# Factorization-machine attention on one core: first and final products of a pair group in one pass of eight 64-row by 32-column products, the finals carried through the relu as a positive and a negative part, and six SyncE tiles in place of seven

## The reference, cut to what matters

```python
B, N_DENSE, N_FIELDS, VOCAB, EMBED_DIM, ATT_DIM = (2048, 13, 26, 12500, 32, 8)
FIRST, SECOND = np.triu_indices(N_FIELDS, k=1)                  # 325 pairs of fields
emb = jax.vmap(lambda tbl, idx: tbl[idx], in_axes=(0, 1), out_axes=1)(embed_tables, sparse)
bi = emb[:, FIRST, :] * emb[:, SECOND, :]                       # pair products, 32 values each
a = jax.nn.relu(jnp.einsum('bpd,dh->bph', bi, att_w_w) + att_w_b)
scores = jnp.einsum('bph,ho->bpo', a, att_d_w) + att_d_b
att_weight = jax.nn.softmax(scores, axis=1)
att_out = jnp.sum(att_weight * bi, axis=1)
x = jnp.concatenate([att_out, dense], axis=-1)
out = jax.nn.sigmoid(x @ fin_w + fin_b)
```

## Time and profile before

| what | value |
|---|---|
| median of 3 runs | 469.24 us (468.34 to 469.72) |
| profiled execution | 468.43 us |
| its span (first to last instruction) | 466.6 us |
| granted TensorE clock, mean | 0.955 |
| busy PE, PEld, DVE | 399.1, 223.0, 395.3 us |
| busy ACT, POOL | 129.7, 332.4 us |
| POOL gathers | 345 indirect DMAs |
| SP row DMAs | 896 |

### The profile page before, as it was taken

The page is one execution under the profiler, slowest core; times in us unless marked ns, Lnnn a source line. Parts: engine busy times, 40 slices in busy tenths (PEclk is TensorE's granted clock), DMA queues, the critical chain, the costliest instruction groups (busy, mean ns, idle before and its releaser), DMA issues.

```text
span 466.6 us, 9661 instructions
## 1 busy us (share of the span) xinstructions
PE 399.1 (86%) x2508; PEld 223.0 (48%) x2508; DVE 395.3 (85%) x641; ACT 129.7 (28%) x302; POOL 332.4 (71%) x349
## 2 busy tenths in 40 slices
PE   1696969999898987899898899699998899699674
PEld 1585746544336654354326766345326755352121
DVE  4999798999768886999795988899796997898765
ACT  3203311242342111142352121042263111125163
POOL 5877777777777777777777777777777777777600
PEclk9978879999999999799999999899999999899988
DMA  8558323222222222232112243323112223322200
GB/s 294 90 151 161 26 13 26 17 26 15 14 15 26 27 15 26 14 26 16 15 15 15 28 22 27 15 26 16 15 15 14 14 13 17 13 16 16 14 1 1
DMA packets 16535, 15.46 MB, mean 33 GB/s; under 512 B 8192, under 2 KB 15584, under 8 KB 16096
## 3 DMA queue, kind: packets, MB, share of 16 engines
q0 software_dynamic: 11040, 5.67, 23.0%
q1 hardware_dynamic: 3056, 6.80, 4.2%
q10 hardware_dynamic: 2384, 2.37, 2.1%
HBM read 14.79 MB, written 0.02 MB: 32 GB/s over the span
## 4 chain that ended last, share of the span: by engine, by line
SPq 69%; issue 25%; PE 2%; DVE 2%; DMA 1%; ACT 1%; ACTq 0%
SPq L401 56%; SPq L397 13%; DMA index<-look_index 1%; PE sums_s L506 1%; DVE ring L850 1%; PE sums_f L492 0%; PE first L482 0%; ACT shared L682 0%; DMA emb_placed<-tables 0%; PE back L530 0%; PE back L522 0%; SPq L379 0%; ACT shared L607 0%; ACT shared L622 0%; ACT shared L601 0%
## 5 line engine op out<-in xcount | busy, mean ns | idle before, releaser
L431 POOL DMA_INDIRECT emb<-tables,rows x300 | 283.7, 946 | 91.5 <-issue 90.6
L850 DVE TENSOR_TENSOR ring<-emb_t,turned 128x512 f32<-128x512 f32 (+9 forms) x180 | 191.7, 1099 | 0.3
L465 PE MATMUL looked_own<-look_parts,onehot 128*128 128x448 f32 x546 | 125.8, 383 | 9.4 <-DVE look_masked L835 4.5
L465 PEld LDWEIGHTS looked_own<-look_parts,onehot 128*128 128x128 f32 x546 | 104.1, 195 | 39.2 <-issue 22.5
L482 PE MATMUL first<-ring,par 128*32 128x512 f32 (+1 forms) x672 | 89.2, 608 | 29.6 <-DVE ring L850 29.0
L594 ACT ACTIVATE hidden<-first,par 128x512 f32<-128x512 f32 (+1 forms) x84 | 56.5, 677 | 175.7 <-PE first L482 175.2
L492 PE MATMUL sums_f<-ring,par 128*32 128x512 f32 (+1 forms) x672 | 89.0, 598 | 0.0
L465 PE MATMUL back<-look_parts,onehot 128*128 128x448 f32 x350 | 79.8, 380 | 10.1 <-DVE onehot L750 6.1
L465 PEld LDWEIGHTS back<-look_parts,onehot 128*128 128x128 f32 x350 | 65.9, 194 | 29.6 <-issue 14.4
L750 DVE TENSOR_TENSOR onehot<-chunk_of,turned 128x896 fp32r<-128x896 f16 x60 | 63.1, 1052 | 0.0
L826 DVE STREAM_TRANSPOSE emb_t<-emb 128x128 f32<-128x128 f32 x100 | 29.9, 302 | 35.0 <-DMA emb<-tables,rows 19.2
(11 more groups left out here) (75 smaller groups left out, 134.2 us busy)
## 6 DMA issues: line engine op xcount, KB each, us to landing
emb_placed<-tables SPq DMA_DIRECT2D x896, 0.1 KB
emb<-tables,rows POOLq DMA_INDIRECT x300, 3.5
ring<-tables SPq DMA_DIRECT2D x2, 1568.0 KB, 9.7
shared<-tables SPq DMA_DIRECT2D x1, 1568.0 KB, 7.8
chunk_of<-chunk_numbers ACTq DMA_DIRECT2D x12, 128.0 KB, 3.6
ring<-tables SPq DMA_DIRECT2D x1, 896.0 KB, 5.9
emb<-tables,rows_first POOLq DMA_INDIRECT x44, 3.8
ring<-tables SPq DMA_DIRECT2D x1, 672.0 KB, 7.3
```

Of the source, the lines that this page charges most:

```text
L431: pool.indirect_dma_start(emb[:, f, g * D:(g + 1) * D], None, stacked, bass.IndirectOffsetOnAxis(ap=row, axis=0), element_offset=at,).then ...
L465: mm = nc.tensor.matmul(looked_rows[look_bank[tile]], onehot[:, tile % ONEHOTS, c, :], look_parts[:, n, c, k, :], start=c == 0 and k == 0, ...
L850: nc.vector.tensor_tensor(slot[:, at:at + n, :], emb_t[:, i:i + n, :], turned[f % 2][:, 0, :].unsqueeze(1).broadcast_to((P, n, P)), ALU.mu ...
```

## The change

**Products.** The contraction of 128 partitions is split in two halves of 64 (`ROW_TILES`), each with two of the four blocks. One half needs 2 x 8 columns of `att_w`, and the 32 columns of a tile have room for two finals a block: one with `fin_w`, one with its negative (the sign is put in by DVE, `weights`, once). The relu of the two are the positive and the negative part of the final, and the score products take their difference beside the scores (`d`, K = 128). So a group is eight products of 64 rows by 32 columns over two `first` banks (of three), two relus of 128x512, and no final products. `sums` replaces `sums_s` and `sums_f`: a batch of up to four groups is one bank, filled in two passes (one a half), copied once (`copy_second`), turned back once (`turn_back`) and taken home in two ACT instructions. DVE's copy L905 is gone. `score` and `final` now lie with the four tiles innermost, so that what reads one tile's pairs steps over four values.

**Buffers.** The ring has 3 slots (4 before) and is free after the first products. `hidden` has 5 places of two halves. Raw tables lie in `hidden` and `ring`. `SHARED_LAST` is 10 (14 before), by its formula with 80 in place of 144 pairs.

**SP and POOL.** `TILES_SP` is (1, 2, 2, 1): 768 row DMAs, and 346 gathers on POOL.

```diff
-RING = 4
-HIDDEN = 6
+RING = 3
+HIDDEN = 5
 BATCH = 4
+FIRST_BANKS = 3
-TILES_SP = (1, 2, 2, 2)
+TILES_SP = (1, 2, 2, 1)
...
-    SHARED_LAST = next(f for f in range(F) if f * (f + 1) // 2 >= (GROUPS_B + 1) * PAIRS_G) - 3
+    SHARED_LAST = next(f for f in range(F) if f * (f + 1) // 2 >= (BATCH + 1) * PAIRS_G) - 3
...
+    batch_ends = [*range(BATCH - 1, GROUPS - 4, BATCH), GROUPS - 4, GROUPS - 1]
...
+        score, final = (cut.rearrange("p (e g) -> p g e", g=G) for cut in (score_all, final_all))
...
                 def first_products(gr):
                     pe.wait_ge(pieces_done, q * PIECES + pieces_through_group(gr))
-                    if gr >= 2:
-                        pe.wait_ge(relu_done, q * GROUPS + (gr - 1))
-                    if gr == 1 and q:
-                        pe.wait_ge(final_done, q * BANKS)
+                    if unit(q, gr, ROW_TILES - 1) >= FIRST_BANKS:
+                        pe.wait_ge(relu_done, unit(q, gr, ROW_TILES - 1) - FIRST_BANKS + 1)
                     n = pairs_c(gr)
                     for j in range(COL_TILES):
-                        mm = nc.tensor.matmul(first[gr % 2][j * TILE:(j + 1) * TILE, 0:n * P], w,
-                                              ring[:, gr % RING, 0:n, j, :], start=True, stop=True)
+                        for r in range(ROW_TILES):
+                            rows_r = slice(r * ROWS_T, (r + 1) * ROWS_T)
+                            mm = nc.tensor.matmul(
+                                first[unit(q, gr, r) % FIRST_BANKS][j * TILE:(j + 1) * TILE, 0:n * P],
+                                weights[rows_r],
+                                ring[rows_r, gr % RING, 0:n, j, :], start=True, stop=True)
                     mm.then_inc(first_done, 1)
...
+                    for r in range(ROW_TILES):
+                        for e, gr in enumerate(groups):
+                            cut = slice(0, pairs_c(gr) * P)
+                            mm = nc.tensor.matmul(sums[e * TILE:(e + 1) * TILE, cut], d_sel[:, r, :],
+                                                  hidden[:, gr % HIDDEN, r, cut], start=r == 0, stop=r == ROW_TILES - 1,
+                                                  skip_group_check=True)
...
+                    for r in range(ROW_TILES):
+                        nc.scalar.activation(hidden[:, gr % HIDDEN, r, cut], first[unit(q, gr, r) % FIRST_BANKS][:, cut],
+                                             ACT.Relu, bias=par[:, cols["bias_a"]]).then_inc(relu_done, 1)
...
-                        dve.wait_ge(finals_done, q * GROUPS + (gr - RING + 1))
+                        dve.wait_ge(first_done, q * GROUPS + (gr - RING + 1))
...
-                dve.wait_ge(finals_done, (q + 1) * GROUPS)
-                dve.wait_ge(back_f_done, q * BANKS + FULL)
-                nc.vector.tensor_copy(second_f[:], sums_f[:]).then_inc(second_f_end_done, 1)
```

More of the change, by code:

```diff
@@ L120, in attention_fm @@
     assert SP_FIELD not in LOOK
-    assert G * D == P and B % (P * G) == 0 and RING < GROUPS and 1 < END_GROUPS
+    assert G * D == P and B % (P * G) == 0 and RING < GROUPS
     pieces = []
@@ L497, in score_products @@
-                def score_products(batch):
-                    first_gr, end = batch_ends[batch - 1] + 1 if batch else 0, batch_ends[batch]
-                    n = first_gr // GROUPS_B
-                    pe.wait_ge(relu_done, q * GROUPS + (end + 1))
-                    if first_gr % GROUPS_B == 0 and n:
-                        pe.wait_ge(second_s_done, q * BANKS + n)
-                    for gr in range(first_gr, end + 1):
-                        tile, half = place(gr) // 2, place(gr) % 2
-                        cut = slice(0, pairs_c(gr) * P)
-                        mm = nc.tensor.matmul(sums_s[tile * TILE:(tile + 1) * TILE, cut], d_sel[:, half, :],
-                                              hidden[:, gr % HIDDEN, cut], start=half == 0,
-                                              stop=half == 1 or gr >= FULL * GROUPS_B, skip_group_check=True)
-                    mm.then_inc(scores_done, 1)
@@ L523, in finals_back @@
-                    mm.then_inc(back_f_done, 1)
-                def scores_back(n):
-                    pe.wait_ge(second_s_done, q * BANKS + (n + 1))
-                    if n < FULL:
-                        pe.wait_ge(final_done, q * BANKS + (n + 1))
-                    for c in range(PAIRS_C):
-                        mm = nc.tensor.transpose(back[:, c, :], second_s[:, c * P:(c + 1) * P], ident)
-                    mm.then_inc(back_s_done, 1)
+                        mm = nc.tensor.transpose(back[:, c, :], second[batch % 2][:, c * P:(c + 1) * P], ident)
@@ L618, in finals_home @@
+                def finals_home(batch):
+                    groups = batch_groups(batch)
+                    whole = len(groups) - (batch == BATCHES - 1)
+                    mv = nc.scalar.activation(pairs_of(final_all, groups[0], whole), in_bank(1, slice(0, whole)), ACT.Copy)
+                    if batch == BATCHES - 1:
+                        mv = nc.scalar.activation(end_pairs(final_all), in_bank(1, whole)[:, 0:LAST_C], ACT.Copy)
                     mv.then_inc(final_done, 1)
-                def scores_home(n):
-                    act.wait_ge(back_s_done, q * BANKS + (n + 1))
-                    nc.scalar.activation(pairs_of(score, n * GROUPS_B, GROUPS_B), scores_in_bank(every),
-                                         ACT.Copy).then_inc(score_done, 1)
```

252 lines of the change are left out of this document (114 added, 138 removed).

## The result

The changed kernel takes 510.85 us (median of four runs, 509.51 to 511.42), the kernel before 469.28 (four runs). The ratio is 1.0885, with a 95% interval of 1.0858 to 1.0912. The forecast was 471.6 with a range to 477.5: the sign was right, the size was not. The profiled execution has a span of 509.6 us, 43.0 more than before, and a mean granted clock of 0.888 where it was 0.955.

What follows compares the result with a forecast made beforehand. POOL's row of gathers was taken as the floor, with DVE returning to it each quad. Field 23 +1.7, chain +3.15, SP wait -4.00, boundaries +1.5 make +2.35 on 468.43: 470.8, as median 471.6; range 470 to 474, slow case to 477.5.

Steps and rivals of the forecast that it cites:

- SP and POOL: Quad 3, field 24: SP's 4.00 us wait goes, gathers come 1.25 us later; a faster rival (0.18) has -2.75.
- the prices of the products: PE and ACT steps: eight small products 1.25 us a group, two score passes 1.9, two relus 1.28.
- the drain: PE, between first and score products: changing tiling mode drains the array, twelve switches a quad; counted at nothing.
- who is waited for: Gather waits of quad 3 nearly vanish from 6.2; DVE waits some 8 us before its last score copies, 7 at quads' ends.
- two signs that were to prove the prediction wrong: Quad 3's gather waits staying above 3 us, or ACT not being what the late first products wait for.
- the ends of the quads before: Ends of quads 0 to 2: 8.0 us later each, 7.5 hidden, 0.5 through at three boundaries, 1.5 in all.
- cover: Idle time hiding each quad end's delay: six gather waits, 6.2 us, plus the gathers' shift of 1.25, together 7.5.
- X: Start of field 23's transpose in quad 3: 437.95 by gathers, 438.7 by DVE's chain; 1.7 us later in the sum.
- the chain of quad 3: From field 23's transpose to the late maximum: 23.0 us, where 19.85 without the SP wait before; +3.15.
- half clock: Rival: gaps slow PE to 1.2 GHz in tail and lookups, 477; chance 0.15, shared with products running four at a time.
- ACT's order: Tail of quad 3: batch and four early exponentials (2 us to 452.95) run ahead of three relu pairs.
- the stride: Reads of scores at a 16-byte step: at most 0.7 ns an element, at most 1 us in the tail.

## Why the prediction was right or wrong

**Right: SP and POOL.** The wait for field 24's rows is gone, SP's last row is issued at 380.6 (forecast: near 381), and the last gather starts at 441.63 for the 441.3 forecast. That closeness is partly luck: in the runs with the same gathers it starts anywhere from 441.16 to 443.82. Alone the line gives 4.6 us where the sum gave 2.75, since the wait it removes had slowed PE behind it too.

**Right: the prices of the products.** Eight small products take 1.09 us (forecast 1.25, bound 1.07). Two passes of scores take 1.92 and a relu pair 1.26, as taken. None of these made the loss.

**Wrong reading, small: the drain.** It was counted at nothing, because score products followed first products or turning back at the usual 0.86. In the kernel before, score and first products have the same tile shape, so those rows hold no change of mode; and where the shape does change, the next work is later: a lookup starts 0.97 us after final products (287.40 to 288.37), first or final products 0.86 to 0.88 after each other. In the changed kernel score products start 1.02 us after the eight first products (442.51 to 443.53), before 0.88 after the four. So a switch costs at most some 0.15 us, an estimate from these starts, or 1.8 a quad of PE's time. No run separates it from what eight small products cost.

**Right in kind: who is waited for.** Gather waits nearly vanish (3.4 us), late first products wait for ACT, and the last copy of scores waits for PE, 9.73 us where about 8 was forecast. At the ends of the other quads the same wait is 10.2 to 10.7, where about 7 was. Neither of the two signs that were to prove the prediction wrong appeared, though it missed by 39 us: one asks for gather waits in quad 3 and the other who delays PE, and neither how long the ends become.

**Wrong: "the ends of the quads before" spent one cover twice.** The step compared a lag of 8.0 us with a cover of 7.5 and let 0.5 through. The single bank was worked out in quad 3 only, as 1.9 us for X, and not at all in quads 0 to 2. But quads 1 to 3 have both the bank and the late end ahead of them, and one set of gather waits to hide them. In the kernel before, the bank used up 10.6 of 19.2 us of that cover and cost nothing. In the changed kernel the cover was gone, and it cost 22.1; that this is twice 10.6 says that the delay is also larger there, with relu pairs and a lookup of 5.57 us for 4.53. Quad 0 is a case of its own: it had 0.8 us of gather waits to spend, the bank cost it 1.0, and its late end came through. X came at 476.04 where the sum had 440.2, so 35.8 of the 40.6 us by which the span was missed lie ahead of it. The prediction had priced lost cover at 8.0 a quad; quads 0 to 2 measured 15.3, 13.6 and 12.8.

The end itself was also too short in the sum. For quad 2 it took 25.2 us from field 24 to the late maximum, and 32.8 were measured (367.22 to 399.98). Its stated terms don't even give the 25.2: the chain of quad 3 has 19.1 from its field 24 (441.85 to 460.95), and with 3.1 for the lookup that is 22.2. With 22.2 the lag would have been 5.0, inside the cover, so the 0.5 that came through rests on a slip. In the run the lookup took 3.4 to 3.8 us, not 3.1, behind scores at half clock.

**Wrong: half clock was a rival, not part of the sum.** Each wait that the sum set for PE was also a gap, and behind the gaps the chain runs slow. The rows for it were there, and the rival gave it 0.15 and 477. Extra matmuls alone took back 10.8 us. The rival's test ("when the lag of a quad's end passes 7.5") was the right one, and the lag passed it: the ends alone grew by 9.3 to 11.0 us.

**Wrong in size: the chain of quad 3.** The last stretch of the timeline of the changed kernel:

```profile
476.04 0.32 DVE L787 STREAM_TRANSPOSE turned<-emb 128x128 f32<-128x128 f32 x1
...
492.27 1.96 PE L473 MATMUL first<-ring,weights 64*32 64x512 f32 x16 [3.12 <-ACT hidden L560]
...
497.25 3.63 PE L487 MATMUL sums<-hidden,par 128*32 128x512 f32 x12 [0.98 <-ACT hidden L560]
...
501.68 1.12 PE L500 MATMUL back<-par,shared 128*128 128x128 f32 x4 [0.80 <-ACT shared L567]
502.84 0.29 DVE L871 COPY shared<-back 128x128 f32<-128x128 f32 x1 [9.73 <-PE back L500]
503.33 0.64 DVE L876 TENSOR_REDUCE neg_max_late<-shared 128x4 f32<-128x276 f32 x1
```

From X to the late maximum it is 27.3 us, not 23.0. The three PE steps take 6.7 where 1.25, 1.8 and 0.66 were taken: 3.0 of the 4.3. The four exponentials add 1.0.

**Wrong in size: ACT's order.** The steps of the tail name it (exponentials ahead of the relu of 18), but it was priced as ACT's own time. The move of one call was worth 11.1 us, since the gap behind it lowers the clock of what follows.

**Wrong bound: the stride.** It was bounded by the earlier trace rows at 0.7 ns an element. Measured are 0.8 on the early reduce (0.81 us for 1024) and 1.0 on an exponential (0.26 us for 256). Over the kernel that came to some 3.5 us, by two runs. The Trainium skill (SBUF — State Buffer, Door 1: The DMA port swizzle) says that an access that crosses to a new 16-byte line pays a penalty, and that a stride of four fp32 is still free. The rows agree with the first and not with the second: a step of four fp32 is 16 bytes, and it pays.

## What to carry to other kernels

List what each idle time of the binding engine hides, and subtract every new delay of the same stretch from it once, in every repetition of the loop. When the cover runs out, delays add up, and gaps of PE in the chain then lengthen its steps too. So put the half-clock duration into the sum for every PE step behind a gap like those here (3.1 to 3.5 us), and order ACT so that what PE waits for comes first. A change in parts should be costed and run in parts: the one-line part was a gain of 4.6 us inside a loss of 41.6.

## What the runs showed of the hardware that was not expected

- Matmuls that nobody reads made a kernel faster by 10.8 us (510.85 to 500.02), by keeping the granted clock up (0.888 to 0.921).
- Eight fp32 products of 64 rows by 32 columns, 512 wide, take 1.09 us, where four of 128 rows by 32 take 1.04 to 1.07: by these times all eight run side by side. The next work of PE starts 1.02 us after the eight, and 0.86 to 0.88 after the four.
- A stride of four fp32 costs 67% on a DVE reduce (2032 for 1220 ns) and 50% on an ACT exponential (758 for 503 ns).
